# Ramp of a fused attention and MLP kernel: paired loads, statistics per tile, three weight splits on GpSimd, two normalisations on ScalarE, another order for V

## The reference

```python
x = L0_attn_x                                   # (4, 512, 512)
xn = _layernorm(x, axis=-1)                     # (x - mean) / sqrt(var + 1e-5)
s = _L0_attn_ref(xn, wq, wk, wv, wo)            # q, k, v = xn @ w.T; rope; decayed linear attention
                                                # in chunks of 64, 16 heads on 4 kv heads; out projection
g = _silu(_L0_ffn_ref(xn, gate_w, up_w, down_w, gate_scale, up_scale, down_scale))
# _L0_ffn_ref: down(silu(gate(xn) * gate_scale) * (up(xn) * up_scale)) * down_scale,
# each weight as w.astype(float8_e4m3fn).astype(float32)
x = x + s * g
```

## Time and profile before

| | us |
|---|---|
| median of 3 runs | 897.44 (897.30 to 897.68) |
| the profiled execution | 898.68 |
| its span, first to last instruction | 896.9 |
| PE busy in it | 889.6 |
| VectorE busy | 656.1 |
| ScalarE busy | 409.5 |
| GpSimd busy | 370.4 |
| mean granted clock of PE | 0.998 |

### The profile page before, as it was taken

How to read it: one execution, slowest core, us unless ns; L and a number is a source line. 1 busy time by engine, 2 the same in 40 slices (tenths; PEclk the granted TensorE clock), 3 DMA queues, 4 the chain that set the end, 5 groups by cost and what they waited for, 6 DMA issues and landing times.

```text
span 896.9 us, 12455 instructions
## 1 busy us (share of the span) xinstructions
PE 889.6 (99%) x4060; PEld 735.0 (82%) x4060; DVE 656.1 (73%) x941; ACT 409.5 (46%) x683; POOL 370.4 (41%) x273
## 2 busy tenths in 40 slices
PE   8999999999999999999999999999999999999998
PEld 5888888888888888888888888888888888888887
DVE  6988896787643257766777867677767678788798
ACT  2544343443533455445355454463554544634442
POOL 1012112122122475536545456365454563553546
PEclk9999999999999999999999999999999999999999
DMA  6694414389650534522544614345335064273854
GB/s 215 187 390 167 171 48 164 141 307 328 244 211 1 212 125 147 186 80 108 187 126 156 220 39 175 102 175 194 101 144 181 18 221 160 99 259 103 295 135 169
DMA packets 86922, 150.08 MB, mean 167 GB/s; under 512 B 38480, under 2 KB 59616, under 8 KB 81504
## 3 DMA queue, kind: packets, MB, share of 16 engines
q1 hardware_dynamic: 86880, 149.55, 48.7%
HBM read 103.38 MB, written 46.15 MB: 167 GB/s over the span
## 4 chain that ended last, share of the span: by engine, by line
PE 91%; issue 3%; DVE 3%; POOL 2%; DMA 0%; ACT 0%; SPq 0%; DVEq 0%; POOLq 0%; ACTq 0%
PE bank L1372 90%; POOL d_r L1308 1%; POOL rot L1317 1%; DMA stage<-in_x_nat 0%; PE bank L1392 0%; DVE d_sb L1164 0%; DVE tail_sb L1217 0%; DVE d_sb L1116 0%; DVE tail_sb L1215 0%; DVE d_r L1191 0%; PE bank L1428 0%; DVE acc L1211 0%; PE bank L1408 0%; DVE o_r L1170 0%; DVE tail_sb L1201 0%
## 5 line engine op out<-in xcount | busy, mean ns | idle before, releaser
L1372 PE MATMUL bank<-xn,aw 128*128 128x512 f32 x960 | 229.1, 390 | 0.0
L1317 POOL TENSOR_TENSOR rot<-rot 128x512 f32<-128x512 f32 x80 | 126.7, 1583 | 233.4 <-DVE rot L1103 233.4
L1372 PEld LDWEIGHTS bank<-xn,aw 128*128 128x128 f32 x960 | 179.0, 188 | 37.4 <-issue 0.7
L1372 PE MATMUL bank<-o_r,ow 128*128 128x512 f32 (+1 forms) x792 | 184.5, 383 | 0.2 <-DVE o_r L1170 0.2
L1308 POOL TENSOR_TENSOR d_r<-d_sb,d_r 128x512 fp32r<-128x512 f32 x126 | 165.5, 1336 | 37.0 <-ACT d_r L762 36.9
L1372 PE MATMUL bank<-xn,gu_w 128*128 128x512 f32 x768 | 179.6, 389 | 0.0
L1372 PEld LDWEIGHTS bank<-o_r,ow 128*128 128x128 f32 x792 | 145.5, 188 | 29.8 <-issue 0.6
L1372 PEld LDWEIGHTS bank<-xn,gu_w 128*128 128x128 f32 x768 | 144.2, 188 | 29.9
L1102 DVE TENSOR_TENSOR rot<-bank,rope 128x512 f32<-128x512 f32 x80 | 55.2, 690 | 100.2 <-ACT rot L747 100.1
L746 ACT COPY rot<-bank 64x512 f32<-64x512 f32 x80 | 46.8, 584 | 156.9 <-PE bank L1372 156.6
L762 ACT CAST d_r<-d_sb 128x512 fp32r<-128x512 f32 x128 | 78.9, 621 | 83.2 <-DVE d_sb L1164 60.7
(11 more groups left out here) (91 smaller groups left out, 948.9 us busy)
## 6 DMA issues: line engine op xcount, KB each, us to landing
xn<-xn_split SPq DMA_DIRECT2D x15, 2048.0 KB, 7.8
v_decayed<-vd_split SPq DMA_DIRECT2D x32, 512.0 KB, 3.2
vd_r<-v_decayed SPq DMA_DIRECT2D x16, 1024.0 KB, 7.0
v_r<-v_split SPq DMA_DIRECT2D x16, 512.0 KB, 3.5
wst<-in_mlp_w SPq DMA_DIRECT2D x10, 768.0 KB, 6.6
xn_split<-xn SPq DMA_DIRECT2D x3, 2048.0 KB, 13.3
stage<-in_x_t SPq DMA_DIRECT2D x20, 256.0 KB, 5.0
stage<-in_attn_w SPq DMA_DIRECT2D x4, 1280.0 KB, 5.5
```

What stands on the lines that cost most here:

```text
L1317: pool.tensor_tensor(rot1[:, r % RRING, :], rot1[:, r % RRING, :], rot2[:, r % RRING, :], ALU.add).then_inc(qk_sum, 1)
L1372: last = pe.matmul(dst, a, b, start=start and x == 0, stop=stop and x == len(pairs) - 1)
```

## The change

- x is loaded in pairs of tiles (512 KB, `load_pair`), V's weights in two halves (`load_wv`). The pair 0, 1 comes first, then ident, both halves of V's weights, and then the other pairs.
- LGROUPS gets tile 0 and tile 1 as groups of their own: mean_var, power and inv_std are done for each, so that later groups have a number one higher: tiles 2 and 3 are group 2, tiles 4 to 7 group 3.
- `wv_split_lo` for slabs 1, 2 and 3 goes from VectorE to GpSimd, slab 1 behind power(1), slabs 2 and 3 behind power(2). Slab 0 stays on VectorE.
- Tiles 6 and 7 are normalised on ScalarE (`norm` there, ON_ACT), from `nmr`, minus mean times rstd, which one more small VectorE instruction makes.
- The four warm-up matmuls ahead of V go, WARM becomes 17. `v_first_low` follows `v_first_high` tile by tile for tiles 0 and 1, ahead of the transposes of tiles 2 and 3, and `v_first_rest` goes over the slabs k first, all four tiles for each.
- V's first ring has six slots, and slabs m = 1 and 2 of the MLP's weights have buffers of their own in place of `mag` (`mag_of`, `spare`). Slab 2's gate and up parts are rounded ahead of slab 1's down part (FLOW, READY), slab 2 is loaded without a wait for a store, and slab 3 behind x tiles 8 to 11.

`w_out` is cut in two for it, `w_out_gu` and `w_out_down`.

The diff, without declarations and the places that only follow from these:

```diff
-LGROUPS = [(0, 2), (2, 4), (4, 8), (8, 12), (12, 16)]
+LGROUPS = [(0, 1), (1, 2), (2, 4), (4, 8), (8, 12), (12, 16)]
...
-VFIRST = 4
+VFIRST = 6
+VUSES = [(2 * TT - r + VFIRST - 1) // VFIRST for r in range(VFIRST)]
...
+SIGNAL = [NAT[i] // 2 * 2 if i < 2 * TT else NAT[i] for i in range(len(NAT))]
+LANDED = [len({j // 2 if j < 2 * TT else j for j in range(i + 1) if SIGNAL[j] == SIGNAL[i]}) for i in range(len(NAT))]
...
-GROUP_AT = {3: 2, 6: 3}
+GROUP_AT = {3: 4, 6: 5}
...
 AW_FROM = 6
-WARM = 14
-WARM_MORE = 4
+WARM = 17
+ON_ACT = (2 * TT - 2, 2 * TT - 1)
+FLOW = [0, 1, 2, 3, 4, 6, 5] + list(range(7, NPIECES))
+READY = [(0, 0), (0, 1), (1, 0), (1, 1), (0, 2), (2, 1), (1, 2), (2, 2)] + [(m, part) for m in range(3, MT) for part in (1, 2)]
...
+        start = ExitStack()
+        kept = sb("kept", [P, 2, KT, S], scope=start)
+        spare = sb("spare", [P, 2, WHOLE], scope=start)
+        start.close()
...
         def ready(m, down=False):
 
-            if m < SLABS:
-                return 2 * SLABS + m + 1 if down else 2 * m + 2
-            return PARTS * SLABS + 2 * (m - SLABS) + (2 if down else 1)
+            return READY.index((m, 2 if down else 1)) + 1
...
+            def load_pair(i):
+
+                if i >= XRING:
+                    sp.wait_ge(ln_t, i - XRING + 2)
+                sp.dma_start(stage[:, NAT[i]:NAT[i] + 2, :], x_nat[ORDER[i // TT], :, i % TT:i % TT + 2, :]).then_inc(x_in[SIGNAL[i]], 16)
+
+            def load_wv(half):
+                sp.dma_start(wv_raw[:, 2 * half:2 * half + 2, :], wv_tab[:, 2 * half:2 * half + 2, :]).then_inc(wv_in[half], 16)
...
-            for i in range(TT):
-                load_x(i)
+            load_pair(0)
             sp.dma_start(ident[:], ident_in).then_inc(ident_sem, 16)
-            for k in range(KT):
-                sp.dma_start(wv_raw[:, k, :], wv_tab[:, k, :]).then_inc(wv_in[k], 16)
-            for i in range(TT, 2 * TT):
-                load_x(i)
+            load_wv(0)
+            load_wv(1)
+            for i in range(2, 2 * TT, 2):
+                load_pair(i)
             load_piece(0)
             load_piece(1)
             sp.dma_start(scale_sb[:], scales).then_inc(const_in, 16)
             sp.dma_start(k_decay[:], k_decay_tab).then_inc(k_decay_in, 16)
             for q in range(2, SLABS * PARTS):
                 load_piece(q)
-            store_v(0)
             load_w(2)
-            for v in range(1, TT + 1):
-                store_v(v)
-            load_w(3)
-            for v in range(TT + 1, 2 * TT):
+            for v in range(TT + 2):
                 store_v(v)
             for i in range(2 * TT, 3 * TT):
                 load_x(i)
+            load_w(3)
+            for v in range(TT + 2, 2 * TT):
+                store_v(v)
...
+            def norm(i):
+                c = ON_ACT.index(i)
+                act.wait_ge(nmr_d, 1)
+                act.activation(stage[:, i % XRING, :], stage[:, i % XRING, :], ACT.Identity,
+                               bias=nmr[:, c:c + 1], scale=rstd[:, i:i + 1]).then_inc(normed_act, 1)
...
             def wv_split_hi(k):
-                act.wait_ge(wv_in[k], 16)
+                act.wait_ge(wv_in[k // 2], 16)
...
             def v_round(v):
 
                 act.wait_ge(v_d, v + 1)
                 r, use = v_ring(v)
+                if v == TT:
+                    act.wait_ge(wv_lo, 1)
+                    act.wait_ge(wv_lo_p, KT - 1)
...
-            wv_split_hi(0)
-            norm_hi(0)
-            for k in range(1, KT):
+            for k in range(KT):
                 wv_split_hi(k)
-            for i in range(1, TT):
+            for i in range(TT):
                 norm_hi(i)
-            for v in range(TT):
-                v_round(v)
-            for i in range(TT, 2 * TT):
-                norm_hi(i)
+            norm(2 * TT - 2)
+            norm(2 * TT - 1)
+            norm_hi(TT)
+            norm_hi(TT + 1)
+            v_round(0)
+            v_round(1)
+            norm_hi(TT + 2)
+            norm_hi(TT + 3)
+            v_round(2)
+            v_round(3)
             act.wait_ge(floor_c, 1)
             w_floor(0)
             w_floor(1)
@@ -678,14 +712,14 @@
             w_floor(2)
             w_floor(3)
             v_round(TT + 2)
+            w_floor(4)
             v_round(TT + 3)
-            w_floor(4)
             act.wait_ge(const_in, 16)
             silu_gate(0, 0)
+            w_floor(6)
             fuse_hi(0)
             w_floor(5)
             silu_gate(1, 0)
-            w_floor(6)
...
+                if i1 == 2 * TT:
+                    dve.wait_ge(rstd_d, grp + 1)
+                    dve.scalar_tensor_tensor(out=nmr[:], in0=mv[:, i1 - 2:i1, 0], scalar=-1.0, in1=rstd[:, i1 - 2:i1],
+                                             op0=ALU.mult, op1=ALU.mult).then_inc(nmr_d, 1)
...
             dve.memset(acc[:, 0, 0, :], 0.0).then_inc(warm_d, 1)
             tile_stats(0)
+            mean_var(0)
             tile_stats(1)
-            mean_var(0)
-            tile_stats(2)
+            mean_var(1)
             inv_std(0)
             norm(0)
+            inv_std(1)
             norm(1)
+            tile_stats(2)
+            norm_lo(0)
             tile_stats(3)
-            mean_var(1)
-            norm_lo(0)
-            inv_std(1)
+            mean_var(2)
+            norm_lo(1)
+            inv_std(2)
             norm(2)
             norm(3)
-            norm_lo(1)
             wv_split_lo(0)
-            wv_split_lo(1)
             norm_lo(2)
             norm_lo(3)
-            wv_split_lo(2)
-            wv_split_lo(3)
             for i in range(TT, 2 * TT):
                 tile_stats(i)
-            mean_var(2)
-            inv_std(2)
-            for i in range(TT, 2 * TT):
-                norm(i)
+            mean_var(3)
+            inv_std(3)
+            norm(TT)
+            norm(TT + 1)
+            norm_lo(TT)
+            norm_lo(TT + 1)
             v_rest(0)
-            for i in range(TT, 2 * TT):
-                norm_lo(i)
+            norm_lo(TT + 2)
+            norm_lo(TT + 3)
             w_exponent(0)
             w_exponent(1)
             for v in range(1, TT):
                 v_rest(v)
             w_round(0)
             w_round(1)
-            v_rest(TT)
             w_exponent(2)
             w_exponent(3)
+            v_rest(TT)
+            w_exponent(4)
             v_rest(TT + 1)
             w_round(2)
             w_round(3)
-            w_exponent(4)
-            for v in range(TT + 2, 2 * TT):
-                v_rest(v)
+            w_exponent(6)
             w_round(4)
             dve.wait_ge(const_in, 16)
             fuse(0, 0)
             w_exponent(5)
+            v_rest(TT + 2)
+            w_minus(6)
+            fuse(1, 0)
+            w_out_gu(6)
+            v_rest(TT + 3)
+            fuse(0, 1)
             w_round(5)
-            w_exponent(6)
-            fuse(1, 0)
-            for m in range(1, MT):
-                if m == 1:
-                    w_minus(PARTS * SLABS)
-                    fuse(0, 1)
-                    w_out(PARTS * SLABS)
-                else:
-                    if m + 1 < MT:
-                        w_round(PARTS * SLABS + m + 1 - SLABS)
-                    fuse(0, m)
+            w_out_down(6)
+            w_exponent(7)
+            fuse(1, 1)
+            for m in range(2, MT):
+                if m + 1 < MT:
+                    w_round(PARTS * SLABS + m + 1 - SLABS)
+                fuse(0, m)
                 if m + 2 < MT:
                     w_exponent(PARTS * SLABS + m + 2 - SLABS)
                 if m - 1 in GROUP_AT:
...
+            def wv_split_lo(k):
+                pool.wait_ge(wv_hi, k + 1)
+                pool.tensor_tensor(wv[:, 1, k, :], wv_raw[:, k, :], wv[:, 0, k, :].bitcast(F32), ALU.subtract).then_inc(wv_lo_p, 1)
+
             power(0)
             power(1)
+            wv_split_lo(1)
             power(2)
+            wv_split_lo(2)
+            wv_split_lo(3)
+            power(3)
...
-            def v_first_rest(v):
-
-                if v == 0:
-                    pe.wait_ge(wv_lo, KT)
-                v_part(v, (1,), end=1).then_inc(v_d, 1)
+            def v_first_rest(k, tiles=range(TT)):
+
+                if k == 0:
+                    pe.wait_ge(wv_lo, 1)
+                else:
+                    pe.wait_ge(wv_lo_p, k)
+                for v in tiles:
+                    mm = pe.matmul(v_bank(v)[:], xn_of(0)[:, 0, k, bass.ts(v, P)], wv[:, 1, k, :], start=False, stop=k == KT - 1)
+                    if k == KT - 1:
+                        mm.then_inc(v_d, 1)
...
             def ln_transpose(i):
-                pe.wait_ge(normed, i + 1)
+                if i in ON_ACT:
+                    pe.wait_ge(normed_act, ON_ACT.index(i) + 1)
+                else:
+                    pe.wait_ge(normed, i + 1)
...
             pe.wait_ge(ident_sem, 16)
             ln_transpose(0)
             ln_transpose(1)
```

(9 more changed lines are left out.)

78 lines of the change are left out of this document (44 added, 34 removed).

## The result

| | before | changed |
|---|---|---|
| median of the comparison, 6 runs each | 897.64 | 901.82 (899.93 to 902.10) |
| ratio, 95% interval | | 1.0041 (1.0030 to 1.0051) |
| the profiled execution, its span | 898.68, 896.9 | 902.04, 900.0 |
| gate stage starts in that trace | 37.09 | 38.33 |

The forecast was 899.8 with 901.4 as its upper end. The sign is right, but the size was too small: 2.4 was forecast, 4.2 was measured, and 901.82 lies 0.4 above the upper end.

What follows compares the result with a forecast made beforehand. PE was taken to bound the kernel. GpSimd's holds on VectorE put the gate stage at 39.4, 2.3 later, so the profiled 898.68 became 901.0; less 1.24 for standing over the median, 899.8, range 896.8 to 901.4.

Steps and rivals of the forecast that it cites:

- The hold on inv_std(2): Ahead of tile 2's transposes, two small VectorE instructions wait for GpSimd's splits 2 and 3: 1.3 each, 2.6 us.
- (b): Only one GpSimd split stands in inv_std(2)'s way: 1.3 less on VectorE, 1.1 on PE, 898.7 us; chance 0.13.
- (c): GpSimd doesn't hold VectorE, gate stage at 36.7: 897.1 us, or 896.3 with the clock kept up; chance 0.20.
- The hold on inv_std(1): Ahead of V's first product, tile 1's inv_std on VectorE waits for GpSimd's wv_split_lo(1): 1.3 us, ending at 10.8.
- inv_std(0)'s second instruction: In tile 0's normalisation, this small VectorE instruction finds GpSimd in power(1) and waits until 8.2.
- V's first product: PE's first V matmul, queued behind tile 1's transposes, starts at 12.3, 0.9 later than before; without them near 10.6.
- Tile 2's transposes: On PE after the first sixteen V matmuls, the transposes of tiles 2 and 3 run from 18.0 to 18.9.
- the gate stage: PE's gate and up products start at 39.4, 2.3 later than the 37.09 of the kernel before.
- The base: The traced execution of the kernel before, 898.68 us, became 901.0; its 1.24 over the median was taken off, giving 899.8.
- Rival (a): PE's clock falls to half again after its pause from 16.1: up to 1.7 us, 900.4 to 901.5; chance 0.26.
- gu_w of m = 2: In the gate stage, these rounded weights are ready near 49.6 and wanted at 53.9: no second stall.
- SP's order: On SP's queue, x loads 8 to 11 go ahead of m = 3's weights, which are not later for it.

Runs made afterwards that it cites:

- e1_ahead: The changed kernel with GpSimd making all three of its splits of V's weights ahead of power(2), not two of them behind it: 898.81 us, ratio 1.0012.
- d_pool: The kernel before with only the splits of V's weight slabs 2 and 3 moved to GpSimd, behind the power of tiles 2 and 3: 898.70 us, ratio 1.0008.
- b_again: The kernel before, unchanged, run once more for a second trace, in one execution: 897.41 us, gate stage at 35.86.
- h_pairs: The kernel before with x loaded in pairs of tiles and V's weights in halves, in its own order of loads: 898.04 us, ratio 1.0008.
- a_again: The changed kernel as it is, run once more for a second trace, in five executions: 900.93 us, ratio 1.0040.
- g_best: The changed kernel with norm_hi(0) between ScalarE's casts, norm_lo(0) ahead of tiles 2 and 3's statistics, GpSimd's splits 2 and 3 after tile 3's normalisation: 897.59 us.
- i_single: g_best with tiles of x and slabs of V's weights loaded one by one again, same bytes and order: 896.99 us, ratio 0.9991.
- e3_third: The changed kernel with one more GpSimd instruction of the split's form behind power(2), written to a free buffer: 903.21 us, ratio 1.0066.

## Why the prediction was right, and where not

**The hold on inv_std(2)** was right in kind and nearly in size: forecast 2.6, near 14.5 and 15.9 with 1.3 each, measured 1.24 and 1.19, 2.4 together, though earlier, at 13.27 and 14.54. Undone (e1_ahead) it gives 2.4 on the time, some 0.5 of it by fewer falls of the clock; alone (d_pool) it costs 1.1, because VectorE has 1.0 of slack there. Rivals (b) and (c) fell.

**The hold on inv_std(1)**, 1.3, failed. The pair landed by 4.64, not 5.2, and the powers of 128x1 took 0.56, where the forecast had 0.71 from a 128x2. And the forecast let power(1) hold inv_std(0)'s second instruction until 8.2; it was not held (0.17 at 6.85, and 0.17 or 0.18 in the eight other traces with that order). By an estimate from these rows, such a hold would have made inv_std(1) 0.5 later, just to where split(1) starts. So tile 1's inv_std was through (8.25) when the cast released split(1) (8.76). V's first product came at 10.53 and 10.98, not 12.3: the value the prediction had named for the case without that hold, 10.6. The Trainium skill's estimate for the pair, 4.0 (page DMA: Bandwidth & Descriptors, section Anatomy of one DMA), was about as far from the measured 4.64 as 5.2 was, on the other side.

**Tile 2's transposes** therefore came 1.0 to 1.4 earlier than the forecast's 18.0, and the gate stage at 38.33 and 38.76, not 39.4.

**The base was wrong, and hid this.** The sum was made against a trace with the half clock in it, and 1.24 was then taken off as if a profiled execution were slower as such. b_again shows that 0.9 of the 1.24 was the clock and 0.34 a later landing, neither of which is there in most executions. Against the usual 35.86, the gate stage is 2.5 to 2.9 later, not 2.3. That the forecast was near on this term is luck, two errors that nearly cancel: a gate stage forecast 0.6 to 1.1 too late, and a base 1.2 too late.

**Rival (a), the clock,** was taken for an alternative, with 0.26. It is a part of the result: about half of the executions have it, for 1.2 (forecast up to 1.7), and it moves the median by some 0.6.

**Priced at nothing and wrong:** the paired loads, 0.24 outside the span (h_pairs); and, in the first trace only, the late waits for stores and loads, with which that execution takes 1.9 longer behind the gate stage than a_again. Together: 2.7 of gate stage, 0.6 of the clock and 0.24 make 3.5 of the 3.6 between the medians of all executions (901.2 and 897.6). The 901.82 of the first six is 0.6 above; four of the six have the fall, and one without it is known to have the late waits (902.04). How many others have them isn't known.

**Priced at nothing and right:** gu_w of m = 2 was ready at 48.4 (forecast 49.6) and wanted 14.5 after 38.33, at 52.8; SP's order brought no wait for weights. What is left of the change once its losses are taken out, step by step, is a kernel 0.6 faster than before, 0.4 of it in the span. The other parts of the change (V's six slots, the spare buffers, two norms on ScalarE, the order of V) were not tested one by one.

| step | us | what is undone |
|---|---|---|
| changed | 901.2 | |
| e1_ahead | 898.8 | the hold on inv_std(2) |
| g_best | 897.6 | ScalarE's four casts ahead of norm_hi(0), and the hold on mean_var |
| i_single | 897.0 | paired loads |

## What to carry to other kernels

Before work goes from VectorE to GpSimd, look at what VectorE does while it runs: behind a GpSimd tensor_tensor of 128x512 (1.26 us), a VectorE instruction of 128x2 with two SBUF inputs costs 1.2 instead of 0.16, and three dependent ones cost three times that where three such GpSimd instructions stand in a row (e3_third). Put the GpSimd work where VectorE reads PSUM or takes statistics, or make it wait until the critical chain is through. Take a second trace of the kernel before, and compare medians of spans over all executions, before a difference of 1 us is explained.
